# Diagonal units of two or three heads issued in turn on different row strips, with a new order of all items

## What is computed

```
xn = layernorm(x)
q3, k3 = xn @ Wq.T, xn @ Wk.T          # 8 heads x 3
v = xn @ Wv.T                          # 8 heads x 16
scores = q3 . k3 * scale + (q3 . dir_h) * (k3 . dir_h)
scores = where(causal, scores, -inf)
attn = softmax(scores)
a = (attn @ v) @ Wo.T
h = bitlinear(xn, w_fc) + gate * (xn @ v.T @ fast_b.T @ u.T)
f = bitlinear(max(h, 0) ** 2, w_proj)  # ternary weights times a scale per row
out = x + a + f
```

## Time and profile before

| | |
|---|---|
| median of 3 runs | 152.54 us |
| lowest and highest | 152.41 and 154.92 us |
| the profiled execution's own time | 153.44 us |
| its span, first to last instruction | 151.6 us |
| PE, PEld busy | 146.6 us, 87.9 us |
| DVE, ACT, POOL busy | 113.9, 113.4, 41.3 us |
| mean granted clock of PE | 0.987 |

### The profile page before, as it was taken

How to read it: one execution, slowest core, us unless ns; L and a number is a source line. 1 busy time by engine, 2 the same in 40 slices (tenths; PEclk the granted TensorE clock), 3 DMA queues, 4 the chain that set the end, 5 groups by cost and what they waited for, 6 DMA issues and landing times.

```text
span 151.6 us, 4295 instructions
## 1 busy us (share of the span) xinstructions
PE 146.6 (97%) x1812; PEld 87.9 (58%) x1812; DVE 113.9 (75%) x266; ACT 113.4 (75%) x243; POOL 41.3 (27%) x59
## 2 busy tenths in 40 slices
PE   7798999999999999999999999999999999999992
PEld 2462887553575564463553928354557358877992
DVE  1999996589999989999999999989733985401222
ACT  3159963497999989889999383998999988697110
POOL 3630283033006150004990010001990243200000
PEclk9999997799999999999999999999999999999999
DMA  4940002401000906101000020100101010101012
GB/s 119 300 115 2 4 0 53 90 2 35 4 0 0 173 4 121 22 0 39 2 2 4 0 69 4 35 6 0 35 4 35 4 35 4 35 4 35 4 35 69
DMA packets 15527, 5.70 MB, mean 38 GB/s; under 512 B 10348, under 2 KB 15380, under 8 KB 15508
## 3 DMA queue, kind: packets, MB, share of 16 engines
q1 hardware_dynamic: 15168, 5.26, 15.0%
q10 hardware_dynamic: 340, 0.17, 0.4%
HBM read 2.02 MB, written 1.05 MB: 20 GB/s over the span
## 4 chain that ended last, share of the span: by engine, by line
PE 89%; DVE 4%; ACT 2%; DMA 2%; POOL 1%; issue 1%; POOLq 0%
PE obank L993 23%; PE bank L888 11%; PE bank L779 10%; PE bank L756 6%; PE bank L895 4%; PE bank L952 4%; PE bank L924 4%; PE bank L956 4%; PE bank L875 3%; PE bank L1003 3%; PE bank L1036 2%; PE bank L849 2%; PE bank L914 2%; DMA x_sb<-in_x 2%; PE bank L959 2%; PE bank L1011 1%
## 5 line engine op out<-in xcount | busy, mean ns | idle before, releaser
L582 DVE TENSOR_REDUCE pm<-bank 128x1 f32<-128x512 f32 (+2 forms) x160 | 90.3, 630 | 9.2 <-PE bank L914 3.8
L699 ACT ACTIVATE Pr<-bank 128x512 f32<-128x512 f32 (+1 forms) x160 | 76.9, 568 | 11.0 <-PE bank L952 5.3
L993 PE MATMUL obank<-Pr,V 128*17 128x128 f32 (+3 forms) x576 | 38.1, 382 | 0.0
L607 DVE TENSOR_TENSOR x_sb<-bank,x_sb 128x256 f32<-128x256 f32 x8 | 3.4, 424 | 20.8 <-PE bank L1036 20.8
L756 PE MATMUL bank<-k_sb 32*128 32x128 bf16 x256 | 18.7, 216 | 0.0
L993 PEld LDWEIGHTS obank<-Pr,V 128*17 128x17 f32 x576 | 12.8, 96 | 9.4 <-issue 5.6
L473 POOL CAST QT<-nmax 128x16 bf16<-128x16 f32 x8 | 2.0, 255 | 58.6 <-DVE nmax L587 58.6
L888 PE MATMUL bank<-xnT,w1T 128*128 128x512 f32 x32 | 17.6, 666 | 0.0
L756 PEld LDWEIGHTS bank<-k_sb 32*128 32x128 bf16 x256 | 14.3, 92 | 5.1 <-ACT Pr L699 1.9
L779 PE MATMUL bank<-w2T,r 128*128 128x128 f32 x128 | 16.2, 280 | 0.0
L779 PEld LDWEIGHTS bank<-w2T,r 128*128 128x128 f32 x128 | 14.9, 192 | 1.2 <-issue 0.8
(11 more groups left out here) (113 smaller groups left out, 189.5 us busy)
## 6 DMA issues: line engine op xcount, KB each, us to landing
out_y<-x_sb SPq DMA_DIRECT2D x8, 128.0 KB, 1.8
x_sb<-in_x SPq DMA_DIRECT2D x3, 256.0 KB, 5.0
wfc_sb<-in_w_fc SPq DMA_DIRECT2D x1, 256.0 KB, 4.6
wpj_sb<-in_w_proj SPq DMA_DIRECT2D x1, 256.0 KB, 3.9
k_sb<-in_consts SPq DMA_DIRECT2D x1, 178.5 KB, 4.3
x_sb<-in_x ACTq DMA_DIRECT2D x1, 128.0 KB, 2.8
x_sb<-in_x SPq DMA_DIRECT2D x1, 128.0 KB, 2.5
vo_sb<-in_vo SPq DMA_DIRECT2D x1, 128.0 KB, 4.2
```

Source lines behind the costliest of these rows:

```text
L582: nc.vector.tensor_reduce(out=dst, in_=src, op=ALU.max, axis=AX.X).then_inc(v_free, 1)
L699: nc.scalar.activation(Pr[:, n % PSLOTS, j, 0:cols], src[:, 0:cols], ACT.Exp).then_inc(a_free, 1)
L993: last = nc.tensor.matmul(obank[32 * h:32 * h + HD + 1, o:o + cols], V[:, at, HG * g + h, :], Pr[:, slot, h, first:first + cols], start=st ...
```

## The change

`MERGE` and `BANKS` are new tables (with as many items of each kind as before), and `JOINS` is a string of 64 digits, one for each diagonal unit in ORDER's sequence. A 1 joins the unit to the one before it. A group of units is then issued at the place of its first member: first PE waits for all their banks and operands, then it issues `late_keys` block by block and within a block head by head, then the scores in the same manner. Each unit of a group has another strip and another bank. The table has 8 groups of three, 11 of two and 18 units alone. A group can mix maxD and stD. DVE and ACT still work on one unit after another, at its own place in ORDER.

`V` becomes a flat row of 8 x 17 numbers and 15 more, which POOL sets to zero; the values are sliced from it by `values`, 17 columns for each head as before.

```diff
-MERGE = ("znzzzzzzzzznwwnnnnlttzzlttezzzzzzztegllzzzziktgtxiimiimmmmzzmzzzmummmmmaggkmuubmmmmimmmemmpkdffsmumm"
...
+MERGE = ("nnnzzzzzzzzzzzzzzwwnntnlttzzezltzztzzgglttikzzzxmliiimmmmmmzzzzmmmuammkemgguubmmmemiimpmmmdfkssssmmm"
...
+JOINS = "0001011011010011001001000100010100010110011001100001001101010110"
...
+DIAGONALS = [x for x in ORDER if x[0] in ("maxD", "stD")]
+JOINED = {x: k == "1" for x, k in zip(DIAGONALS, JOINS)}
...
-        V = sb("V", [P, NT, H, HD + 1])
+        V = sb("V", [P, NT, H * (HD + 1) + HD - 1])
+        heads = V[:, :, 0:H * (HD + 1)].rearrange("p n (h d) -> p n h d", h=H)
...
-            nc.gpsimd.memset(V[:, :, :, HD:HD + 1], 1.0).then_inc(ones_ready, 1)
+            nc.gpsimd.memset(V[:, :, H * (HD + 1):], 0.0).then_inc(ones_ready, 1)
+            nc.gpsimd.memset(heads[:, :, :, HD:HD + 1], 1.0).then_inc(ones_ready, 1)
...
+            def together(x):
+
+                k = DIAGONALS.index(x)
+                n = next((m for m in range(k + 1, len(DIAGONALS)) if not JOINED[DIAGONALS[m]]), len(DIAGONALS))
+                return DIAGONALS[k:n]
+
+            def late_keys(x, i):
...
+                nc.tensor.matmul(at[:, :, i, :], hot[32 * j:32 * j + 32, i, :],
+                                 tri[32 * j:32 * j + 32, by, None, :].to_broadcast([32, TPC, SUB]),
+                                 start=i == 0, stop=False)
+
+            def diagonal(x, n):
+
+                c, j, half = x[1], x[-1], coords(x[1])[2]
+                if x[0] == "maxD":
+                    left, right = queries(c, j, n, ROWS), keys(c, j, half, n * P, P, ROWS)
+                else:
+                    left, right = keys(c, j, half, n * P, P, ROWS), shifted(c, j, n * P, P, ROWS)
+                return nc.tensor.matmul(bank[BANK[x]][:, n * P:(n + 1) * P], left, right, start=False, stop=n == TPC - 1)
...
+                elif kind in ("maxD", "stD") and not JOINED[item]:
                     pe.wait_ge(ld_k, 16)
+                    side_by_side = together(item)
+                    for x in side_by_side:
+                        empty(x)
...
+                    for i in range(NSUB):
+                        for x in side_by_side:
+                            late_keys(x, i)
                     for n in range(TPC):
+                        for x in side_by_side:
+                            last = diagonal(x, n)
+                            if n == TPC - 1 and x[0] == "maxD":
+                                last.then_inc(v_full, 1)
+                            elif n == TPC - 1:
+                                last.then_inc(a_full, 1)
```

More of the change, by code:

```diff
@@ L158, in streams @@
     return s
-MERGE = ("znzzzzzzzzznwwnnnnlttzzlttezzzzzzztegllzzzziktgtxiimiimmmmzzmzzzmummmmmaggkmuubmmmmimmmemmpkdffsmumm"
[L162 to L170, removed]
+MERGE = ("nnnzzzzzzzzzzzzzzwwnntnlttzzezltzztzzgglttikzzzxmliiimmmmmmzzzzmmmuammkemgguubmmmemiimpmmmdfkssssmmm"
+         "mkfuuffmmmmmssvmmssffkkmmmmpffssmmvmmssdumsmssmfmmmvvsmmmsbmmmmesssvsssmmmmvkmmmpfuuufsdmmuussmsmmvv"
+         "sssmmfmmuufmmmussvumsmmsfssmmmvmsssmmmmmsssvmmssbmssssvjsmsmsvpmmdsssmvmmssssovmmmsvsfmmsvssmmsmvssm"
+         "mmvsssmommmsvmssqsmmmfsssmmvjmmssoqqqjpmmssvdmmsssvvmmmmommsssmosmmssmvmsssmmmvsmmmmmsssvsmmsspoosss"
+         "sdvmmssosmmvsmsssssssosssmvvvsmmmsmsvsmmsssvsssmmmmpvmmsssvmsssssvvdsmsmssqmmqqsmmmssvvpsssqssodooss"
+         "sssssovvvvssssssovvvvooohohoo")
+BANKS = ("0121201301203456120345612302615406231416052431605016342520416051342056142360531640236543201651324065"
+         "0146320541634205631045362104532140652613450621430215643025406123465106342501632165403216450235162403"
+         "1524603451260314106523150462541306124560321054365014236241503124650326145032631042631506432105420315"
+         "642034653450261425013602415346015632403425601342561043621462143056126215034430503")
+JOINS = "0001011011010010011001000100010100010110011001100001001101010110"
 def merged():
@@ L684, in _ @@
                     src = filled(item)
-                    nc.scalar.copy(V[:, q * TPC:(q + 1) * TPC, :, 0:HD],
+                    nc.scalar.copy(heads[:, q * TPC:(q + 1) * TPC, :, 0:HD],
                                    src[:, :].rearrange("p (n h d) -> p n h d", h=H, d=HD)).then_inc(a_free, 1)
@@ L749, in shifted, with maxima_turned, values @@
                 return Qm[32 * j:32 * j + rows, c % QMSLOTS, first:first + n]
[L751 to L758, removed]
+            def maxima_turned(c):
+                if c in BY_PE:
+                    pe.wait_ge(a_free, A_FREE[("mT", c)])
+                else:
+                    pe.wait_ge(qm_ready[c], 16)
+            def together(x):
[3 more added lines that the diff above has]
+            def late_keys(x, i):
+                at = bank[BANK[x]][:, :].rearrange("p (n i k) -> p n i k", n=TPC, i=NSUB)
+                j, by = x[-1], 0 if x[0] == "maxD" else 1
+                nc.tensor.matmul(at[:, :, i, :], hot[32 * j:32 * j + 32, i, :],
[5 more added lines that the diff above has]
+                    left, right = queries(c, j, n, ROWS), keys(c, j, half, n * P, P, ROWS)
+                else:
+                    left, right = keys(c, j, half, n * P, P, ROWS), shifted(c, j, n * P, P, ROWS)
+                return nc.tensor.matmul(bank[BANK[x]][:, n * P:(n + 1) * P], left, right, start=False, stop=n == TPC - 1)
+            def values(at, head):
+                return V[:, at, head * (HD + 1):(head + 1) * (HD + 1)]
             def rows_turned(c, half):
@@ L915, in _ @@
                                      stop=True).then_inc(v_full, 1)
[L916 to L919, removed]
+                elif kind in ("maxD", "stD") and not JOINED[item]:
                     pe.wait_ge(ld_k, 16)
-                    late_keys(o, j, 0)
-                    rows_turned(c, half)
-                    for n in range(TPC):
-                        last = nc.tensor.matmul(o[:, n * P:(n + 1) * P], queries(c, j, n, ROWS),
-                                                keys(c, j, half, n * P, P, ROWS), start=False, stop=n == TPC - 1)
-                    last.then_inc(v_full, 1)
+                    side_by_side = together(item)
+                    for x in side_by_side:
+                        empty(x)
+                        if x[0] == "maxD":
+                            rows_turned(x[1], coords(x[1])[2])
+                        else:
+                            maxima_turned(x[1])
+                    for i in range(NSUB):
+                        for x in side_by_side:
+                            late_keys(x, i)
+                    for n in range(TPC):
+                        for x in side_by_side:
[4 more added lines that the diff above has]
+                                last.then_inc(a_full, 1)
                 elif kind == "mT" and item[1] in BY_PE:
@@ L937, in _ @@
                     last.then_inc(a_full, 1)
-                elif kind in ("stD", "stO", "stA", "stB"):
+                elif kind in ("stO", "stA", "stB"):
                     _, c, step, j = item
@@ L941, in _ @@
                     o = empty(item)
[L942 to L949, removed]
+                    maxima_turned(c)
                     if kind == "stO":
@@ L953, in _ @@
                                                 start=True, stop=True)
[L954 to L957, removed]
                     elif kind == "stA":
@@ L992, in _ @@
                         for h in range(HG):
-                            last = nc.tensor.matmul(obank[32 * h:32 * h + HD + 1, o:o + cols], V[:, at, HG * g + h, :],
+                            last = nc.tensor.matmul(obank[32 * h:32 * h + HD + 1, o:o + cols], values(at, HG * g + h),
                                                     Pr[:, slot, h, first:first + cols], start=step == "D" and k == 0,
```

2 lines of the change are left out of this document (1 added, 1 removed).

## The result

The changed kernel takes 150.88 us in the median of its runs (150.67 to 152.96). Its ratio to the kernel before is 0.9891, with a 95% interval of 0.9862 to 0.9919: 1.1% or about 1.7 us faster. I had forecast 149.6 us, 1.9% faster: the direction was right and the size was not. PE's granted clock falls to half near 25 us in some executions, and those with a lower mean clock took 0.2 to 8.5 us more, so "at full clock" means executions whose mean granted clock was 0.997 or more. At full clock the kernel before took 152.47 us (median of nine executions, 151.89 to 152.84) and the changed one 150.67 and 150.80.

The account below looks back on a forecast made before the run. PE was taken as the bound. Terms -4.7 - 0.2 + 1.65 + 0.3 = -2.95 us gave 150.5 from the profiled 153.44; shifted to the median, the forecast was 149.6 us (-1.9%), range 147.6 to 152.6, its own 148.3 to 151.0.

Parts of the forecast that it names:

- PE is the bound: Whole kernel: PE is busy 97% of the span and makes up 89% of the chain that ended last.
- 0.24 us for a further unit, a queue in front of each strip: Consecutive diagonal units: each further one costs 0.24 us, entering once the last three matmuls before it are queued at their strip.
- 27 joins and 4.7 us of strip time: Row-strip stretches on PE: joining 27 of 64 diagonal units cuts counted strip time from 32.7 to 28.0 us.
- Waiting for banks, 1.65 us: Before diagonal groups: 27 banks asked for early bring 2.5 waits more at 0.65 us each, costing 1.65 us.
- DVE's fill, 0.3 us: From 33 to 97 us: nearly full DVE takes back 0.3 us of the gain from the 10 joins there.
- the rival built on it: DVE bounds 33 to 97 us, so only the 17 joins outside count: -2.0, 150.5 us; chance 0.20.
- Issue is the bound (0.18): PE's sequencer delivers one matmul per 30 ns, so joins bring nothing: 152.3 us; chance 0.18.
- Slower (0.06): Groups wait for late banks and hold all behind; with 14 of 19 waiting, +4.2, 156.7 us; chance 0.06.
- The clock (0.14): Near w1: PE's clock fall, expected again, doesn't come, giving 148.3 us; chance 0.14.
- Changes of division, -0.2 us: PE switching between row strips, column strips and full array: 131 stretches become 129, at 0.10 us each, 0.2 us less.
- the order itself, 0: At the start, chunk 1's second to fourth maxD move before ffn(0,1); no PE time saved, counted 0.
- V: 0: Sums over values: the slices read stay the same 17 columns and the added memset is on POOL, so zero.

Follow-up runs that it names:

- e10: Changed kernel with DVE's reductions and ACT's exponentials cut to 128 columns or fewer, PE's work unchanged: 146.55, 147.09 and 147.57 us at full clock.
- e1_alone: Changed kernel with JOINS all zeros, so new order and banks but each diagonal unit issued by itself: 152.19 us at full clock, one execution.
- e12: Changed kernel with w1's products grouped in two blocks and six joins more, 33 of 64: 150.21 us (149.81 to 151.04).
- e7: Changed kernel with w1's eight products issued as four with 128 rows, then four with 16: median 149.15 us, ratio 0.9741 to the kernel before.
- e8: Changed kernel without V's zero tail and its memset: 150.10, 150.51 and 150.84 us at full clock.
- e3: Changed kernel with only the 10 joins between 33 and 97 us: 151.17 to 151.57 us at full clock.
- e5: Changed kernel without joins, DVE reading half the columns of each off-diagonal maximum (maxO): 151.73 us at full clock.
- e9: Changed kernel without joins, DVE's reductions and ACT's exponentials cut to 128 columns or fewer, PE's work unchanged: 149.73 to 150.16 us at full clock.
- e4: Changed kernel with only the 17 joins before 33 us and after 97 us: 151.10 to 151.32 us at full clock.
- e6: Changed kernel with all joins, DVE reading half the columns of each off-diagonal maximum (maxO): 149.82, 150.39 and 150.56 us at full clock.
- e13: Changed kernel with all DVE reductions reading a quarter or fewer of their columns, ACT's work in full: 149.60 to 150.15 us at full clock.
- e14: Changed kernel with ACT's exponentials of 128 columns only, DVE's work in full: 149.29 us at full clock in one execution.
- e11: Kernel before with only w1's products grouped, four with 128 rows then four with 16: ratio 0.9888 (0.9806 to 0.9971).
- e15: Kernel before's order and banks with 38 joins and w1's products grouped: ratio 0.9821 (0.9738 to 0.9904).

## Why the prediction was right or wrong

- **PE is the bound, 0.24 us for a further unit, a queue in front of each strip:** the prices are right, and the queue, which no run here tests by itself, foretold the starts rightly. That PE is the bound is only part of it: with PE's work unchanged and both engines light the kernel is 3.65 us faster (e10), so the wait for single banks bounds it too. Units alone are still 0.242 us apart, a group of two or three lets the next in after 0.25 us, and all its matmuls start within 0.41 us.
- **27 joins and 4.7 us of strip time:** the count fits where it can be seen: stretches in which nothing waits for a bank give the 0.24 us of a join in full. Its sum of 4.7 is a count and was not measured.
- **Waiting for banks, 1.65 us:** this step failed. I priced the waits that joining adds in front of the diagonal units. They did not grow: PE's loads before L774 waited 0.6 us on ACT, where the earlier trace rows has 3.9 in all (0.2 in e1_alone, so the order took them away and the joins added 0.4; idle time with no releaser named went from 1.0 to 3.0 us, but it is 2.7 without the joins too). Nor was 0.65 us the price of such a wait: while its loads stand idle, PE is still busy with the matmuls before, and PE itself shows no wait in front of a diagonal unit. What I left out are the waits behind them. An item further on in the stretch, whose bank comes free at a time that joins don't move, ate the gain. For this order the joins took out 5.1 us and gave back 3.6 (33.1 - 28.0, less 1.45), and not 1.65 and the 0.3 for DVE. In the sum for the whole change, -4.7 - 0.2 and a measured -1.7 leave 3.2 us of waits where I had 1.95. Light engines bring back 1.5 us of the 3.6 (in the stretches behind the start, 1.9 of 2.9), so that part is shown to be the way round of the banks; the cause of the rest stays open.
- **DVE's fill, 0.3 us:** the share rose to 97% (33 to 90 us), as I said it would, and the rival built on it would give 150.5 us, near the measured time. It was still the wrong cause: with 15 us less work on DVE the time moved by 0.35 us. A time that fits a rival doesn't prove it.
- **Issue is the bound (0.18):** refuted, 24 matmuls start in 0.41 us, 17 to 18 ns each. The rule of the Trainium skill that I set against the change (TensorE: Matmul & The Clock Gate, "Wait — 56ns, not 53.3ns?") holds for one strip at most, where this trace has 56 ns at 128 columns; over several strips the measured rate is below its 25 ns.
- **Slower (0.06):** not for the kernel; e12 shows its mechanism near 62 us, where a group of four waits for a bank.
- **The clock (0.14):** I priced the fall at 1.3 us. Before, executions with one fall took 153.34 to 153.96 us where others took 152.47, which is 0.9 to 1.5. In the changed kernel it cost 0.2 us (150.95 against 150.74), and 2.2 in the execution with a mean clock of 0.977 (152.96).
- **Changes of division, -0.2 us, and the order itself, 0:** the order alone, changes of division included, measured -0.3, from one execution. V: 0, as predicted. The own-time sum of -2.95 us on 153.44 would be 150.5; the profiled execution took 150.95.

## What to carry to other kernels

Before shortening work on a bound engine, lay out for each stretch what its last item waits for: if that is a buffer whose release doesn't move with the edit, the stretch keeps its length and the time saved turns into waiting. A high busy share of the engine behind is no proof that it limits; make it lighter and look. And when small matmuls of different row heights alternate, sort them first: that was worth as much here as all the joins.

## What was not expected of the hardware

A change between products with 128 and with 16 rows cost 0.19 us each in w1, more than the 0.10 us of drain between stretches.

What follows w1 matters for how long the clock stays low. This is the window from 24.5 to 34.7 us of e1_alone, then of the changed kernel, then of e7:

```profile
24.50:34.70 10.20, 10.20 (x76) 6.12 (x76) 6.35 (x21) 4.43 (x8) 1.23 (x1) 0.50 0.28 54
```

```profile
24.50:34.70 10.20, 10.02 (x121) 5.16 (x121) 8.66 (x25) 6.95 (x14) 2.26 (x5) 0.83 0.28 54
```

```profile
24.50:34.70 10.20, 9.15 (x122) 4.28 (x120) 9.00 (x26) 6.92 (x14) 2.68 (x5) 1.00 0.35 67
```

The granted clock is 0.50 throughout without the joins, at the level of 1.2 GHz, 0.83 on average with them and 1.00 with w1 grouped; before each of them PE had run w1, in turn in the first two and in blocks in the third. That the dense groups behind w1 end the low stretch earlier, and that a denser w1 prevents it, fits these three profiles, but a profile isn't the rule: e8, with all the joins, was at half for 10.2 us in its own. The counts say more. A mean clock of 0.964 to 0.967, which is such a long fall in each of the five profiles that have it, came in 18 of the 27 executions without joins near w1 (e1, e3, e5, e9), in 4 of the 44 with them and w1 in turn (the changed kernel, e4, e6, e8, e10, e13, e14), and in none of the 12 with w1 grouped (e7, e12). In the old order e11 and e15 had one fall each with w1 grouped, so w1 isn't the only cause. While the clock was at half, a round of three took 0.107 us and not 0.056: the groups slow down with the clock in full.
